# v by seven block products of 256 columns, with the pieces of Wv split once and kept in memory

## What is computed

```python
q = jnp.einsum('bnd,ed->bne', neuron_states, Wq)
k = jnp.einsum('bnd,ed->bne', neuron_states, Wk)
v = jnp.einsum('bnd,ed->bne', neuron_states, Wv)
rel = jnp.einsum('bnd,bmd->bnm', q, k)
rel = adjacency.T[None, :, :] * rel
rel = rel / jnp.linalg.norm(rel, axis=2, keepdims=True)
return jnp.einsum('bnm,bmd->bnd', rel, v)
```

## Time and profile before

| what | value |
|---|---|
| median of 3 runs | 1996.67 us (1995.74 to 1997.96) |
| the profiled execution's own time | 1996.92 us |
| its span, first to last instruction | 1994.9 us |
| PE busy | 1974.0 us, 99% of the span |
| PEld, DVE, POOL, ACT busy | 82%, 72%, 46%, 35% |
| mean granted clock of TensorE | 0.997 of full speed (2.4 GHz) |

### The profile page before, as it was taken

The page is one execution under the profiler, slowest core; times in us unless marked ns, Lnnn a source line. Parts: engine busy times, 40 slices in busy tenths (PEclk is TensorE's granted clock), DMA queues, the critical chain, the costliest instruction groups (busy, mean ns, idle before and its releaser), DMA issues.

```text
span 1994.9 us, 26073 instructions
## 1 busy us (share of the span) xinstructions
PE 1974.0 (99%) x8688; PEld 1633.5 (82%) x8688; DVE 1443.7 (72%) x2195; ACT 702.8 (35%) x1011; POOL 918.5 (46%) x631
## 2 busy tenths in 40 slices
PE   6999999999999999999999999999999999999998
PEld 5888888888888888888888888888888888888887
DVE  7686777767777677777767777767686777767775
ACT  5333333334333342323424233342333433334331
POOL 3634526445353543436434373442634526445351
PEclk8999999999999999999999999999999999999999
DMA  7434342333424344242443423343333342333401
GB/s 264 168 122 142 142 147 100 136 127 144 161 84 150 113 152 152 103 157 93 158 142 146 138 105 132 135 154 126 126 121 142 142 148 100 137 126 145 160 21 63
DMA packets 78797, 265.46 MB, mean 133 GB/s; under 512 B 7360, under 2 KB 7360, under 8 KB 74432
## 3 DMA queue, kind: packets, MB, share of 16 engines
q1 hardware_dynamic: 78784, 265.32, 37.0%
HBM read 225.97 MB, written 39.32 MB: 133 GB/s over the span
## 4 chain that ended last, share of the span: by engine, by line
PE 98%; DVE 1%; DMA 1%; issue 0%; SPq 0%; ACT 0%; POOLq 0%; POOL 0%; DVEq 0%
PE banks L357 33%; PE banks L359 33%; PE banks L358 33%; DMA scr<-xT 1%; DVE x_lo L623 0%; SPq L288 0%; SPq L287 0%; ACT x_hi L484 0%; DVE res L790 0%; DVE stats L793 0%; DVE aw L652 0%; DVE rel L639 0%; POOLq L54 0%; DVE res L802 0%; POOL rstd L923 0%
## 5 line engine op out<-in xcount | busy, mean ns | idle before, releaser
L357 PE MATMUL banks<-yv 128*128 128x512 f32 x1024 | 398.3, 389 | 0.0
L358 PE MATMUL banks<-yv 128*128 128x512 f32 x1024 | 398.3, 389 | 0.0
L359 PE MATMUL banks<-yv 128*128 128x512 f32 x1024 | 398.3, 389 | 0.0
L906 POOL TENSOR_TENSOR square_sum<-square_sum,squares 128x512 f32<-128x512 f32 x224 | 319.5, 1426 | 87.1 <-ACT squares L565 76.6
L357 PE MATMUL banks<-yv,x_hi 128*128 128x512 f32 x896 | 348.5, 389 | 0.0
L358 PE MATMUL banks<-yv,x_hi 128*128 128x512 f32 x896 | 348.5, 389 | 0.0
L359 PE MATMUL banks<-yv,x_lo 128*128 128x512 f32 x896 | 348.5, 389 | 0.0
L923 POOL TENSOR_TENSOR rstd<-var_eps,minus_half 128x1 f32<-128x1 f32 x128 | 130.3, 1018 | 335.6 <-DVE var_eps L797 335.6
L565 ACT ACTIVATE squares<-rel 128x512 f32<-128x512 f32 x224 | 140.0, 632 | 270.5 <-POOL rel L899 99.4
L359 PEld LDWEIGHTS banks<-yv 128*128 128x128 f32 x1024 | 192.2, 188 | 39.9
L357 PEld LDWEIGHTS banks<-yv 128*128 128x128 f32 x1024 | 192.2, 188 | 39.9
(11 more groups left out here) (77 smaller groups left out, 2992.3 us busy)
## 6 DMA issues: line engine op xcount, KB each, us to landing
scr<-adj SPq DMA_DIRECT2D x128, 512.0 KB, 5.8
aw<-a_kept SPq DMA_DIRECT2D x15, 3584.0 KB, 11.1
scr<-xT SPq DMA_DIRECT2D x32, 1024.0 KB, 7.2
res<-x SPq DMA_DIRECT2D x128, 256.0 KB, 2.7
aw<-w_kept SPq DMA_DIRECT2D x16, 2048.0 KB, 7.9
out<-res SPq DMA_DIRECT2D x128, 256.0 KB, 2.0
a_kept<-aw SPq DMA_DIRECT2D x1, 3584.0 KB, 11.9
w_kept<-yv SPq DMA_DIRECT2D x2, 1024.0 KB, 5.0
```

The source lines that it names most:

```text
L357: pe.matmul(bank_ap, l_hi, r_hi, start=first and i == 0, stop=False, skip_group_check=on)
L358: pe.matmul(bank_ap, l_hi, r_lo, start=False, stop=False, skip_group_check=on)
L359: mm = pe.matmul(bank_ap, l_lo, r_hi, start=False, stop=i == len(pairs) - 1, skip_group_check=on)
L906: pool.tensor_tensor(square_sum[:, h, :], square_sum[:, h, :], squares[:, n % SQRING, :], ALU.add).then_inc(square_added, 1)
```

## The change

v = x Wv' is made by seven block products as well, in the order `V_ROUNDS`. A product works on two pairs of row tiles (i), each of two tiles (h), with 2 blocks of the contraction and 3 matmuls of 256 columns; a pair's two halves share one PSUM bank. ScalarE copies the first product out (`v_copy`), DVE forms the blocks (`v_sum`), and both split them (`v_hi_piece`, `v_lo_piece`) in the order of `V_BLOCKS`: (0,0), (1,1), (1,0), (0,1). The first output tile takes v's row tiles in the order 4 to 7, 0 to 3. X21 is no longer split. On DVE the transposes (`turn_squares`) stand after block (0,0), and the third chunk and `norms` behind all of v. Wv's seven pieces (four of them sums) are split once, on ScalarE and POOL, in four slots of 256 columns by two, and stored one by one around the first batch's y; 14 banks of them are fetched into `aw` in each batch, in place of 8. The stores of A's pieces and the first loads of `res` move into the first batch. The sums S1 to S4 of x are as before.

```diff
-X11, X12, X22, S1, S2, S3, S4, X21 = range(8)
+X11, X12, X22, S1, S2, S3, S4 = range(7)
...
+V_ROUNDS = (1, 6, 2, 7, 5, 4, 3)
+
+X_PIECES = (X22, X11, X12, S1, S3, S2, S4)
...
-        wv_hi = aw[:, 0:4 * BANK].rearrange("p (k e) -> p k e", k=KD)
-        wv_lo = aw[:, 4 * BANK:8 * BANK].rearrange("p (k e) -> p k e", k=KD)
+        wv_hi, wv_lo = a_hi, a_lo
...
-        def v_bank(m):
-            return bank[(2 + m) % 8]
+
+        v_bank = {"a": (bank[2], bank[3]), "c": (bank[4], bank[5]), "b": (bank[6], bank[7])}
+        v_p1_raw, v_u2_raw = [v_raw[:, i, :] for i in range(2)], [v_raw[:, 2 + i, :] for i in range(2)]
+        v_c22_raw = [square_sum[:, i, :] for i in range(2)]
...
+        WV_PIECES = (B11, B21, B22, T1, T3, T2, T4)
+        WV_SUMS = (T1, T3, T2, T4)
+        wv_slot = [squares[:, :, :], square_sum[:, :, :], v_raw[:, 0:2, :], v_raw[:, 2:4, :]]
...
-            for t in range(RRING):
-                load_res(0, t)
-            sp.wait_ge(wv_split, 2)
-            sp.dma_start(w_kept_v[:, 0:KD, :], wv_hi0.bitcast(F32)).then_inc(w_stored, DMA)
-            sp.dma_start(w_kept_v[:, KD:2 * KD, :], wv_lo0.bitcast(F32)).then_inc(w_stored, DMA)
-            sp.wait_ge(a_split, 7)
-            sp.dma_start(a_kept, aw[:, :].bitcast(F32)).then_inc(a_stored, DMA)
+
+            def store_wv(i):
+                sp.wait_ge(wv_split, i + 1)
+                sp.dma_start(w_kept_v[:, WV_PIECES[i], :, :], wv_slot[i % WSLOTS]).then_inc(w_stored[i % WSLOTS], DMA)
+
+            for i in range(3):
+                store_wv(i)
...
+                if first:
+                    sp.wait_ge(a_split, 7)
+                    sp.dma_start(a_kept, aw[:, :].bitcast(F32)).then_inc(a_stored, DMA)
+                    for i in range(3, 7):
+                        store_wv(i)
+                    for t in range(RRING):
+                        load_res(0, t)
+                    for i in range(WSLOTS):
+                        sp.wait_ge(w_stored[i], 2 * DMA if i < 3 else DMA)
+                    sp.wait_ge(a_stored, DMA)
 
                 sp.wait_ge(y_done, b * Y_COUNT + Y_COUNT)
-                sp.wait_ge(w_stored, 2 * DMA)
-                sp.wait_ge(a_stored, DMA)
-                sp.dma_start(aw[:, 0:8 * BANK].bitcast(F32), w_kept).then_inc(w_loaded, DMA)
+                sp.dma_start(aw[:, :].bitcast(F32), w_kept).then_inc(w_loaded, DMA)
...
-                for m in range(MT):
-                    if m < 2:
-                        pe.wait_ge(s_c12, b * HT + (m + 1))
-                    elif m < 4:
-                        pe.wait_ge(s_m11, b * HT + (m + 1))
-                    elif m < 6:
-                        pe.wait_ge(s_c21, b * HT + (m - 1))
-                    else:
-                        pe.wait_ge(s_c12, b * HT + (m - 3))
-                    blocks = (X11, X12) if m < HT else (X21, X22)
-                    product(v_bank(m),
-                            [((x_hi[:, blocks[k // 2], k % 2, cols(m % HT)], x_lo[:, blocks[k // 2], k % 2, cols(m % HT)]),
-                              (wv_hi[:, k, :], wv_lo[:, k, :])) for k in range(KD)],
-                            True).then_inc(v_done, 1)
+                for k in V_ROUNDS:
+                    left, right = LEFT[k], RIGHT[k]
+                    for i in range(2):
+                        if k == 1:
+                            pe.wait_ge(s_c12, b * HT + (i + 1))
+                        if k == 6:
+                            pe.wait_ge(s_m11, b * HT + (2 + i + 1))
+                        if k == 5:
+                            pe.wait_ge(s_c21, b * HT + (2 + i + 1))
+                        if k == 2:
+                            pe.wait_ge(v_p1, b * 2 + (i + 1))
+                        if k == 7:
+                            pe.wait_ge(v_u2, b * 2 + (i + 1))
+                        if k == 4:
+                            pe.wait_ge(v_r, b * 2 + (i + 1))
+                        if k == 3:
+                            pe.wait_ge(v_c22, b * 2 + (i + 1))
+
+                        into = pair_of(v_bank[s_into[k]][i])
+                        for h in range(2):
+                            rows = cols(2 * i + h)
+                            mm = product(into[:, h, :],
+                                         [((x_hi[:, left, d, rows], x_lo[:, left, d, rows]),
+                                           (wv_hi[:, right, d, :], wv_lo[:, right, d, :])) for d in range(2)],
+                                         k in (1, 6, 5) and h == 0)
+                        mm.then_inc(v_done, 1)
...
+                v_order = (4, 5, 6, 7, 0, 1, 2, 3)
                 for t in range(MT):
                     c = t % CRING
                     if t < 2:
-                        pe.wait_ge(v_split, b * MT + (7 + t))
+                        pe.wait_ge(s_c12, b * HT + (2 + t + 1))
                     pe.wait_ge(chunk_split, b * MT + (t + 1))
                     ready = None
                     if t == 0:
-                        ready = [(v_split, b * MT + (m + 1)) for m in range(MT)]
+                        ready = [(v_split, b * MT + (5 + n // 2)) for n in range(MT)]
...
+                             for m in v_order], True, ready).then_inc(o_done, 1)
...
+                if first:
+                    for i in range(3, 7):
+                        wv_hi_piece(i)
...
+            def v_copy(b, i):
+                act.wait_ge(v_done, v_count(b, 1, i))
+                act.activation(v_p1_raw[i], v_bank["a"][i], ACT.Copy).then_inc(v_p1, 1)
+
+            def v_hi_piece(b, block, i):
+                if block == (0, 0):
+                    act.wait_ge(v_done, v_count(b, 2, i))
+                    source = v_bank["a"][i]
+                if block == (1, 1):
+                    act.wait_ge(v_c22, b * 2 + (i + 1))
+                    source = v_c22_raw[i]
+                if block == (1, 0):
+                    act.wait_ge(v_c21, b * 2 + (i + 1))
+                    source = v_p1_raw[i]
+                if block == (0, 1):
+                    act.wait_ge(v_c12, b * 2 + (i + 1))
+                    source = v_u2_raw[i]
+                act.activation(v_block(v_hi, *block, i), pair_of(source), ACT.Copy).then_inc(v_hi_made, 1)
...
+                    for i in range(WSLOTS):
+                        act.wait_ge(w_stored[i], 2 * DMA if i < 3 else DMA)
...
+                for name, i in square_order[6:SQUARES - 1]:
                     square(b, name, i)
-                for m in range(MT):
-                    v_piece(b, m)
-                    if m in (1, 2):
-                        chunk(b, m - 1)
+                v_copy(b, 0)
+                square(b, *square_order[SQUARES - 1])
+                v_copy(b, 1)
+                chunk(b, 0)
+                v_hi_piece(b, (0, 0), 0)
+                chunk(b, 1)
+                v_hi_piece(b, (0, 0), 1)
                 chunk(b, 2)
-                if not last:
-                    act.wait_ge(v_done, b * MT + MT)
+                for block in V_BLOCKS[1:]:
+                    for i in range(2):
+                        v_hi_piece(b, block, i)
...
+            def v_lo_piece(b, block, i, source):
+                dve.wait_ge(v_hi_made, b * 8 + (2 * V_BLOCKS.index(block) + i + 1))
+                dve.tensor_tensor(v_block(v_lo, *block, i), pair_of(source), v_block(v_hi, *block, i).bitcast(F32),
                                   ALU.subtract).then_inc(v_split, 1)
+
+            def v_sum(b, k, i):
+                a, bb, c = (v_bank[n][i] for n in ("a", "b", "c"))
+                if k == 6:
+
+                    dve.wait_ge(v_p1, b * 2 + (i + 1))
+                    dve.wait_ge(v_done, v_count(b, 6, i))
+                    dve.tensor_tensor(v_u2_raw[i], c, v_p1_raw[i], ALU.add).then_inc(v_u2, 1)
+                if k == 7:
+
+                    dve.wait_ge(blocks_turned, b * HALVES + (HALVES + HALVES))
+                    dve.wait_ge(v_done, v_count(b, 7, i))
+                    dve.tensor_tensor(v_c22_raw[i], c, v_p1_raw[i], ALU.add).then_inc(v_r, 1)
+                if k == 5:
+
+                    dve.wait_ge(v_r, b * 2 + (i + 1))
+                    dve.wait_ge(v_done, v_count(b, 5, i))
+                    dve.tensor_tensor(v_c22_raw[i], bb, v_c22_raw[i], ALU.add).then_inc(v_c22, 1)
+                if k == 4:
+
+                    dve.wait_ge(v_done, v_count(b, 4, i))
+                    dve.tensor_tensor(v_p1_raw[i], c, v_p1_raw[i], ALU.add).then_inc(v_c21, 1)
+                if k == 3:
+
+                    dve.wait_ge(v_u2, b * 2 + (i + 1))
+                    dve.wait_ge(v_done, v_count(b, 3, i))
+                    dve.tensor_tensor(v_u2_raw[i], bb, v_u2_raw[i], ALU.add).then_inc(v_c12, 1)
...
+            def turn_squares(b):
                 dve.wait_ge(square_added, b * ADDED + (ADDED + SQRING))
                 for h in range(HALVES):
                     dve.transpose(squares[:, h, :], square_sum[:, h, :]).then_inc(blocks_turned, 1)
+
+            def norms(b):
...
```

(46 more changed lines are left out.)

## The result

| what | before | after |
|---|---|---|
| median of 6 runs each, us | 1996.81 | 2032.38 (2031.67 to 2033.58) |
| ratio, 95% interval | | 1.0179 (1.0168 to 1.019) |
| the profiled execution, us | 1996.92 | 2032.82 |
| its span, us | 1994.9 | 2030.8 |
| PE busy | 99% | 97% |

The forecast was 2028, the range 1986 to 2060.

A forecast was written before the change was run, and what follows sets the result against it. The kernel was taken as bound by its matmul columns plus a little per matmul, PE 99% busy. 15 x (3.2 - 1.6) - 1.6 + 9 = +31.4 us on 1996.9 gave 2028 us, range 1986 to 2060.

The forecast's parts named there:

- Pitch of 256 columns: Stage v: 168 matmuls at 0.120 us each (0.1067 columns plus 0.0134) take 20.16 us, a gain of 1.6 us a batch.
- load slot of 0.085 us: On PE in v, a weight load holds its slot an estimated 0.085 us at 2.4 GHz, hidden below 0.107 us of columns.
- Rival (c): In v, weight loads bind at 0.188 us: 2211 us; chance 0.10, shared with any pitch between 0.13 and 0.188.
- (b): In v, a short pitch of 0.109 us, DVE's queue becomes the limit: 2008 us; chance 0.13 with nearby mixes that lose.
- DVE and ScalarE in v: Inside v, no wait stops PE; the last low part is done 2.2 us behind v's end, with 1.9 us over.
- E: The time near which v's last product ends and the outputs start on PE, forecast at 352.60.
- Late norms: Norms behind v delay the power to E + 8.1 and chunk 5 to E + 30.4: 3.2 us lost in 15 batches.
- "no lock" and "lock": Whether X22's low part on DVE holds up GpSimd's power; lock taken, first x sum E + 10.75; without, total 16 us lower.
- Transfers of Wv's pieces: The load of Wv's pieces grows from 2.0 to 3.5 MB, lands in 11.1 us and costs nothing.
- First batch: One-off cost of 9 us: 4 us in DVE's queue and some 5 us at ScalarE's wait; bounds 0 and 16.
- The wait for the stores: In the first batch ScalarE waits until Wv's pieces are stored, about 62; PE needs its copy near 58: some 5 us.
- Rival (a): Faster: if GpSimd's first x sum starts by E + 7.5, PE never waits in the outputs: 1980 us; chance 0.17.

The follow-up runs named there:

- v256: The kernel before with each of v's 512-column matmuls cut into two of 256 columns, nothing else changed; 2017.09 us, ratio 1.0107.
- v128: The kernel before with each of v's matmuls cut into four of 128 columns (384 a batch); 2337.77 us, one execution.
- v64: The kernel before with each of v's matmuls cut into eight of 64 columns (768 a batch); 4247.71 us, one execution.
- norms_back: The changed kernel with norms moved forward on DVE, right behind the transposes, inside v; 2037.23 us, ratio 1.0207.
- half_copies: The changed kernel with 8 of the 16 small copies in norms left out and the last reduction over that half; 2008.78 us, ratio 1.0061.
- act_copies: The changed kernel with norms' first reduction inside v, its 16 small copies on ScalarE, the last reduction behind block (1,0); 1986.91 us, ratio 0.9955.
- s1_first: The changed kernel with X22's low part ahead of norms on DVE, and POOL's sums S1 and S3 ahead of the power; 2044.57 us, ratio 1.024.
- first_wait: The changed kernel with ScalarE's first-batch wait for the stores of Wv's pieces moved from the first s copy to the first square; 2020.37 us, ratio 1.0122.

## Why the prediction came out, step by step

The sum of the prediction was 15 x (3.2 - 1.6) - 1.6 + 9 = 31.4 us; measured in the profiles 15 x (3.24 - 1.61) - 1.6 + 13.1 = 35.9.

- **Pitch of 256 columns: right in the value, wrong in one number behind it.** 0.120 forecast and measured, in after and in v256. My load slot of 0.085 us, half of the 0.17 of the earlier trace rows, is 0.1115 by v128, if it is the load that sets the pitch there. It was still hidden, but with 0.0085 us to spare and not 0.035. A single distance between two starts at the start-up was too weak a row: it is the first pair of loads behind a pause, and at the same clock v64 has 0.2133. Rival (c) also misreads it: what follows a load's start by 0.17 us in the earlier trace rows is the next load; that load's own matmul starts 0.42 behind it. A further cut of the columns gains almost nothing: 128 columns still take 0.1115 us. Rivals (b) and (c) fell both: 0.109 and 0.188 are not seen.
- **DVE and ScalarE in v: right.** No wait of PE there. The last low part of v was done 371.3 - 368.96 = 2.3 us behind E, forecast 2.2.
- **Late norms: right.** The power at E + 8.1 as forecast, S1 at E + 10.65 against 10.75, chunk 5 ready at E + 30.26 against 30.4. The loss was 3.24 a batch, forecast 3.2. norms_back, half_copies and act_copies show each from another side that this chain, and not the load of DVE as a whole, makes it. Of the two ends for the power, "no lock" and "lock", it was the lock: 2.58 us beside X22's low part, 1.65 in the last batch, which has none. How far the lock reaches I had too narrow: s1_first shows that it holds up 32x8 copies with one input as well.
- **Transfers of Wv's pieces: right.** 3.5 MB land in 11.0 us, and no wait on them is listed.
- **First batch: the mis-sized term.** Forecast 9, measured 13.1, made of other parts. The 4 us that POOL's eleven operations were to cost DVE ahead of k = 7 of y didn't come: DVE started those sums at 42.75 against 41.64 and PE did not wait. The wait for the stores was 10.9 us, not 5: they landed near 64.8, not 62, and PE, not delayed in y, was there at 54.4, not 58. The clock behind the gap, which stood only in the bounds, took 2.6. So 4 us too much stood against 8.5 too little, and that 9 came as near to 13.1 is in part luck. first_wait shows that all but 1.1 of it hung on that wait.
- **Rival (a)** put the no-wait case at 1980. act_copies brings that case about, with S1 at E + 5.5: 1986.9. In its trace the first v starts 11.2 us later than before, in place of 9, and a batch gains 1.40 in place of 1.6: 1996.9 - 16 x 1.40 + 11.2 = 1985.7, the time of the profiled execution.

## What to carry to other kernels

Fewer columns pay only if what the new scheme asks of the other engines finds room; cost a moved step by who is queued behind it on every engine, down to the operation that PE waits for. Where DVE and POOL both sit on that path, small copies go to ScalarE even if each takes longer there. A wait that occurs once, in the first batch, cost 13.1 us here, against 48.6 (15 x 3.24) for the late norms of all the others: place it ahead of the instruction that overwrites the buffer, and not ahead of a queue.

## What the runs showed of the hardware that I had not expected

- Matmuls that each have their own load of 128 columns did not come below a pitch of some 0.11 us at full clock (mean 0.1115 with 128 columns in v128, about the same with 64 in v64), or 0.2133 at 1.2 GHz, with 64. A matmul of 256 columns (0.120) is only just above that. That the load sets this floor was not separated from other costs of the pair.
- With 64 columns behind each load, the granted clock fell to 0.50 a few us into the v stage though PE had no idle time, and stayed there (100.00 of 100.00 us busy in the window), and the mean over the span was 0.698. With 128 columns it stayed at 0.998. Why was not tested.
- A 32x8 copy on DVE takes 0.17 us (16 in 3.13), but one that starts while POOL makes a sum of 128x1024 stands until that sum is done (1.34 and 2.34 us in s1_first). On ScalarE it takes 0.215 us beside such sums.
- A one-off gap of 10.9 us on PE costs 2.6 us more by the clock, since the next twelve matmuls run at 1.2 GHz. In norms_back a gap of 2.3 us in v was followed by 3.4 us at a granted clock of 0.50 in six of 16 batches and by none in the other ten.
